# A decoder layer on one core: scores and values' products in blocks of four heads

## What is computed

```
scores = q k^T * scale            (256 x 256)
probs  = softmax(scores)          per row
out_h  = probs v                  (256 x 64)
```

## Time and profile before

| | |
|---|---|
| median of 3 runs | 3596.63 us (3593.33 to 3597.58) |
| the profiled execution | 3596.79 us, its span 3595.0 us, granted TensorE clock 0.993 |
| TensorE busy | 3499.9 us, 97% |
| TensorE weight load | 2955.3 us, 82% |
| VectorE busy | 2361.6 us, 66% |
| ScalarE busy | 2220.9 us, 62% |
| GpSimd busy | 2121.0 us, 59% |

### The profile page before, as it was taken

The page is one execution under the profiler, slowest core; times in us unless marked ns, Lnnn a source line. Parts: engine busy times, 40 slices in busy tenths (PEclk is TensorE's granted clock), DMA queues, the critical chain, the costliest instruction groups (busy, mean ns, idle before and its releaser), DMA issues.

```text
span 3595.0 us, 80997 instructions
## 1 busy us (share of the span) xinstructions
PE 3499.9 (97%) x28992; PEld 2955.3 (82%) x28992; DVE 2361.6 (66%) x7401; ACT 2220.9 (62%) x6442; POOL 2121.0 (59%) x1928
## 2 busy tenths in 40 slices
PE   6899999999999999999999999999999999999997
PEld 5788888888888888888888888888888888888886
DVE  6666667666676666676666666666766666666664
ACT  5666666666666666666665766656666657666563
POOL 5555666555675556665556765566655567655661
PEclk8999999999999999999999999999999999999999
DMA  3100000000000000000000000000000000000000
GB/s 98 37 10 13 10 9 10 10 12 12 7 11 11 9 12 12 6 10 10 12 12 7 13 10 9 12 13 6 10 10 12 12 6 13 10 9 12 13 6 8
DMA packets 46796, 47.44 MB, mean 13 GB/s; under 512 B 8256, under 2 KB 43328, under 8 KB 46400
## 3 DMA queue, kind: packets, MB, share of 16 engines
q1 hardware_dynamic: 45696, 41.99, 4.0%
q10 hardware_dynamic: 704, 0.27, 0.0%
HBM read 33.86 MB, written 8.39 MB: 12 GB/s over the span
## 4 chain that ended last, share of the span: by engine, by line
PE 89%; DVE 6%; issue 2%; POOL 2%; ACT 2%; DMA 0%; ACTq 0%; POOLq 0%; DVEq 0%
PE unit_ps L536 19%; PE pT_ps L648 14%; PE oT_ps L665 14%; PE score_ps L632 11%; PE wo_ps L690 10%; PE unit_ps L546 9%; PE unit_ps L524 9%; DVE x L1021 2%; ACT probs L798 1%; POOL probs L1150 1%; DVE probs L936 1%; PE unit_ps L555 1%; DVE bn L863 1%; DVE x_in L1029 1%; DVE w_lo L851 0%
## 5 line engine op out<-in xcount | busy, mean ns | idle before, releaser
L1150 POOL TENSOR_TENSOR probs<-probs,inv_sum 128x512 f32<-128x512 f32 x1024 | 1062.0, 1041 | 967.3 <-DVE inv_sum L919 967.2
L787 ACT ACTIVATE pT<-pT_ps 128x512 f32<-128x512 f32 x1024 | 605.9, 594 | 135.9 <-PE pT_ps L648 135.4
L798 ACT ACTIVATE probs<-probs,neg_max 128x256 f32<-128x256 f32 x1024 | 508.7, 499 | 277.5 <-DVE probs L936 277.5
L648 PE MATMUL pT_ps<-ident,probs 128*128 128x128 f32 x4096 | 635.3, 280 | 13.0 <-POOL probs L1150 12.4
L648 PEld LDWEIGHTS pT_ps<-ident,probs 128*128 128x128 f32 x4096 | 452.9, 141 | 221.6 <-issue 204.1
L798 ACT ACTIVATE probs<-score_ps,neg_max 128x256 f32<-128x256 f32 x1024 | 476.5, 476 | 179.1 <-DVE neg_max L925 179.1
L665 PE MATMUL oT_ps<-pT,v_sb 128*64 128x256 f32 x4096 | 555.9, 392 | 3.8 <-ACT pT L787 3.5
L936 DVE TENSOR_SCALAR_CACHE_REDUCE probs<-score_ps,mask_add 128x256 f32<-128x256 f32 x1024 | 433.5, 480 | 105.8 <-PE score_ps L632 102.8
L536 PE MATMUL unit_ps<-xs_hi,w_lo 128*128 128x256 f32 x1536 | 460.2, 300 | 8.7 <-DVE swap L972 7.2
L536 PE MATMUL unit_ps<-xs_hi,w_hi 128*128 128x256 f32 x1536 | 436.9, 284 | 0.0
L536 PE MATMUL unit_ps<-xs_lo,w_hi 128*128 128x256 f32 x1536 | 436.3, 284 | 0.0
(11 more groups left out here) (121 smaller groups left out, 8422.2 us busy)
## 6 DMA issues: line engine op xcount, KB each, us to landing
x_in<-dram_x SPq DMA_DIRECT2D x32, 256.0 KB, 2.7
xn<-dram_ctx SPq DMA_DIRECT2D x32, 256.0 KB, 2.7
layer_out<-x SPq DMA_DIRECT2D x32, 256.0 KB, 2.2
swap<-dram_bout SPq DMA_DIRECT2D x32, 128.0 KB, 3.3
rope<-dram_be SPq DMA_DIRECT2D x32, 64.0 KB, 3.1
rope<-dram_we SPq DMA_DIRECT2D x5, 256.0 KB, 2.9
probs<-dram_sk SPq DMA_DIRECT2D x4, 256.0 KB, 4.4
x<-dram_cq SPq DMA_DIRECT2D x4, 256.0 KB, 2.8
```

The costliest lines, as they stand in the source:

```text
L648: last = nc.tensor.transpose(pT_ps[s % 2][:, k * T + t * P:k * T + (t + 1) * P], probs[:, hs % P_BUFS, t, k * P:(k + 1) * P], ident[:])
L787: nc.scalar.activation(flat(pT[:, s % 2, :, :]), pT_ps[s % 2][:], ACT.Copy).then_inc(pT_ready.sem, 1)
L798: last = nc.scalar.activation(dst, src, ACT.Exp, bias=neg_max[:, h % STATS, t:t + 1], scale=1.0 if h < H else -1.0, accum_out=row_sum[:, h ...
L1150: nc.gpsimd.tensor_tensor(weights, weights, inv.unsqueeze(2).to_broadcast([P, NT, T]), ALU.mult).then_inc(probs_ready.sem, 1)
```

## The change

Scores are issued for four heads in a row, in the first slot of each four, and `values` takes the four heads of a group at once, in the slot where the next group's scores are (slots 0, 4, 8, 12, 24, 28, 32, and 17 for the last group of self-attention). `score_ps` and `pT_ps` become four banks `head_ps`: a head's bank holds its scores, and after the exponentials its transposed probabilities. The separate `pT` buffers are gone: ScalarE copies the transposed probabilities back over the head's own `probs`, of which there are 6. So the scores of a head wait for the copy of the head four before it (`pT_ready`), and whoever first writes a `probs` buffer (exponentials of self heads, row maxima of cross heads) waits for the values' product of the head that had it before (`pv_done`). The steps of a head have slots of their own in `AT`, counted within four: row maxima of heads 0, 1, 2 in the first and 3 in the second; exponentials of 0, 1 in the first and 2, 3 in the third; reciprocals and GpSimd's products of 0, 1 in the second and 2, 3 in the third; transposes of 0, 1 at the start of the third and 2, 3 at the start of the fourth. W follows one slot behind the values. All units have new slots and flags, and BI no longer comes right behind scores. Of the removed lines below only some are shown.

```diff
-P_BUFS = 4
+P_BUFS = 6
...
+def in_slot(what, s):
+
+
+    first = s - s % HG
+    return [(head_in(first + j), first + j) for j in range(HG) if AT[what][j] == s % HG and head_in(first + j)]
+
+
+def turned_in(s, end):
+
+
+    first = s - s % HG
+    return [(head_in(first + j), first + j) for j in range(HG)
+            if AT["turned"][j] == 2 * (s % HG) + end and head_in(first + j)]
+
+
 def meets_values(s):
 
 
-    if s % SLOTS == AT["last values"][0]:
-        return head_in(s - 3)
-    if s % 2 or s % SLOTS == AT["last values"][0] + 1:
+    turn, at = divmod(s, SLOTS)
+    if at == AT["last values"][0]:
+        return head_in(turn * SLOTS + DRAIN[0] - HG)
+    if at % HG or at == DRAIN[0]:
         return None
-    return head_in(s - 4)
+    return head_in(s - HG)
+
+
+def leaves(s):
+
+
+    return None if (s - 1) % SLOTS == AT["last values"][0] else meets_values(s - 1)
 
 
 def projects(s):
 
-    if s % SLOTS == AT["last projection"][0]:
-        return head_in(s - 4)
-    pair = meets_values(s - 1)
-    return pair if pair and pair[1] % HG == 2 else None
-
-
-
-
-
-
-
+    turn, at = divmod(s, SLOTS)
+    if at == AT["last projection"][0]:
+        return head_in(turn * SLOTS + DRAIN[0] - HG)
+    behind = s - AT["projected"]
+    return None if behind % SLOTS == AT["last values"][0] else meets_values(behind)
...
 UNITS = {
+    0: [],
+    1: [("Q", 2, 0, NOW), ("V", 0, 0, NOW)],
+    2: [("K", 2, 0, LATE)],
+    4: [],
+    5: [("V", 1, 0, NOW), ("V", 2, 0, NOW), ("Q", 3, 0, LATE)],
+    6: [("L3", 0, -1, LATE)],
+    7: [("K", 3, 0, NOW), ("LG", 0, -1, NOW)],
+    8: [],
+    9: [("V", 3, 0, LATE), ("EX", 0, -1, LATE), ("EX", 1, -1, LATE)],
+    10: [("EX", 2, -1, NOW)],
+    12: [],
+    13: [("EX", 3, -1, LATE)],
+    14: [],
+    15: [("EX", 4, -1, NOW)],
+    17: [("GT", 0, -1, LATE)],
+    18: [("V", 4, 0, LATE), ("K", 4, 0, NOW), ("EX", 5, -1, NOW), ("EX", 6, -1, NOW), ("L2", 0, 0, LATE), ("EX", 7, -1, LATE)],
+    19: [("Q", 4, 0, NOW), ("Q", 5, 0, NOW)],
+    20: [("V", 5, 0, LATE)],
+    21: [("K", 5, 0, NOW), ("BI", 0, -1, NOW)],
+    22: [("Q", 6, 0, NOW)],
+    23: [],
+    24: [("K", 6, 0, LATE)],
+    26: [("V", 6, 0, LATE)],
+    27: [],
+    28: [("L1", 0, 1, LATE), ("K", 7, 0, LATE)],
+    29: [("Q", 0, 1, LATE)],
+    30: [],
+    31: [("K", 0, 1, NOW)],
+    32: [],
+    33: [("Q", 1, 1, NOW), ("V", 7, 0, LATE)],
+    35: [],
...
+    "turn": 1,
+    "split": 2,
+    "statistics 3": 2,
+    "norm 3": 4,
+    "gate table": 9,
+    "context": 16,
+    "mask": 0,
+    "norm 2": [18, 1],
+    "x to x1": 23,
+    "statistics 1": 26,
+    "norm 1": 27,
+    "maxima": [0, 0, 0, 1],
+    "exponentials": [0, 0, 2, 2],
+    "sums": [1, 1, 2, 2],
+    "turned": [4, 4, 6, 6],
+    "projected": 1,
+    "residual 3": 1,
+    "projection first": [14, 27, 31, 35],
...
-        pT = sb("pT", [P, 2, NT, T])
...
-        score_ps = [bank(f"score_ps{i}") for i in range(2)]
-        pT_ps = [bank(f"pT_ps{i}") for i in range(2)]
+
+        head_ps = [bank(f"head_ps{i}") for i in range(HG)]
...
-                back = (0, h - 1) if h else (-1, NH - 1)
-                read = exp_done if 0 < h <= H else max_ready
-                pe.wait_ge(read.sem, read.at(b, back[0], back[1] + 1))
+                back = (0, h - HG) if h >= HG else (-1, NH + h - HG)
+                pe.wait_ge(pT_ready.sem, pT_ready.at(b, back[0], back[1] + 2))
...
+            def turn_probs(b, s, h):
+
+                pe.wait_ge(probs_ready.sem, probs_ready.at(b, 0, h + 1))
                 for k in range(NT):
                     for t in range(NT):
+                        last = nc.tensor.transpose(head_ps[s % HG][:, k * T + t * P:k * T + (t + 1) * P],
+                                                   probs[:, s % P_BUFS, t, k * P:(k + 1) * P], ident[:])
                 last.then_inc(probs_turned.sem, 1)
...
+                g = h // HG
+                pe.wait_ge(pT_ready.sem, pT_ready.at(b, off, h + HG))
+                pe.wait_ge(v_ready.sem, v_ready.at(b, off, g + 1))
+                pe.wait_ge(oT_ready.sem, oT_ready.at(b, off, g))
+                for hl in range(0, HG, 2):
+                    for k in range(NT):
+                        for i in range(2):
+                            last = nc.tensor.matmul(oT_ps[i * HD:(i + 1) * HD, (hl // 2) * T:(hl // 2 + 1) * T],
+                                                    v_sb[:, g % 2, k, (hl + i) * HD:(hl + i + 1) * HD],
+                                                    probs[:, (hs + hl + i) % P_BUFS, k, :], start=k == 0,
+                                                    stop=k == NT - 1, skip_group_check=True)
                 last.then_inc(pv_done.sem, 1)
...
-                    if s % 2 == 0 and head_in(s) and exists(b, 0):
+                    if s % HG == 0 and head_in(s) and exists(b, 0):
                         scores(b, s, head_in(s)[1])
+                        scores(b, s + 2, head_in(s)[1] + 2)
                     if bias_first(s) and exists(b, UNITS[s][0][2]):
                         unit(b, s, 0, *UNITS[s][0][:3])
                     if meets_values(s) and s != AT["last values"][0]:
                         values(b, s)
-                    if head_in(s - 2):
-                        turn_probs(b, s)
+                    for (_, h, _), hs in turned_in(s, 0):
+                        if exists(b, 0):
+                            turn_probs(b, hs, h)
...
-                    act.wait_ge(pv_done.sem, pv_done.at(b, off if g > 1 else off - 1, 2 * ((g - 2) % (2 * NG)) + 2))
+                    act.wait_ge(pv_done.sem, pv_done.at(b, off if g > 1 else off - 1, (g - 2) % (2 * NG) + 1))
...
+            def pT_out(b, s, h):
+
+                act.wait_ge(probs_turned.sem, probs_turned.at(b, 0, h + 1))
+                nc.scalar.activation(flat(probs[:, s % P_BUFS, :, :]), head_ps[s % HG][:],
+                                     ACT.Copy).then_inc(pT_ready.sem, 1)
...
+                    last_group = meets_values(s) if s == AT["last values"][0] else None
+                    if leaves(s) and exists(b, leaves(s)[0]):
+                        oT_out(b, s - 1)
                     for n, (kind, g, off, late) in enumerate(UNITS.get(s - 1, ())):
                         if exists(b, off) and late == LATE:
                             unit(b, unit_ps[unit_bank(s - 1, n) % 2][:], kind, g, off)
-                    if group_ends and s != AT["last values"][0]:
-                        oT_out(b, s)
-                    if here and exists(b, 0):
-                        exponentials(b, s, here[1])
-                    if head_in(s - 2):
-                        pT_out(b, s)
+                    for (_, h, _), hs in in_slot("exponentials", s):
+                        if exists(b, 0):
+                            exponentials(b, hs, h)
+                    for (_, h, _), hs in turned_in(s, 0):
+                        if exists(b, 0):
+                            pT_out(b, hs, h)
...
+                back = buffer_before(s)
+                dve.wait_ge(pv_done.sem, pv_done.at(b, back[0], back[1] // HG + 1))
...
-                    here, summed = head_in(s), head_in(s - 1)
-                    if summed and exists(b, summed[0]):
-                        reciprocal(b, *summed[:2])
-                    if here and s % 2 == 0 and exists(b, 0):
-                        row_maximum(b, s, here[1])
-                        row_maximum(b, s + 1, here[1] + 1)
+                    last_group = meets_values(s) if s == AT["last values"][0] else None
+                    for (_, h, _), hs in in_slot("sums", s):
+                        if exists(b, 0):
+                            reciprocal(b, 0, h)
+                    for (_, h, _), hs in in_slot("maxima", s):
+                        if exists(b, 0):
+                            row_maximum(b, hs, h)
                     for n, (kind, g, off, late) in enumerate(UNITS.get(s - 1, ())):
                         if exists(b, off) and late == LATE:
                             unit(b, unit_ps[unit_bank(s - 1, n) % 2][:], kind, g, off)
-                    pair = meets_values(s)
-                    group_ends = pair and pair[1] % HG == 2 and exists(b, pair[0])
-                    if group_ends and s != AT["last values"][0]:
-                        oT_low(b, s)
+                    if leaves(s) and exists(b, leaves(s)[0]):
+                        oT_low(b, s - 1)
```

More of the change, by code:

```diff
@@ L150 @@
 AT = {
-    "turn": 2,
-    "split": 3,
-    "statistics 3": 4,
-    "norm 3": 5,
+    "turn": 1,
+    "split": 2,
+    "statistics 3": 2,
+    "norm 3": 4,
     "gate weights": 8,
-    "gate table": 8,
-    "context": 11,
-    "mask": 13,
+    "gate table": 9,
+    "context": 16,
+    "mask": 0,
     "statistics 2": [18, 0],
-    "norm 2": [18, 3],
-    "x to x1": 22,
-    "statistics 1": 24,
-    "norm 1": 25,
+    "norm 2": [18, 1],
+    "x to x1": 23,
+    "statistics 1": 26,
+    "norm 1": 27,
     "last values": [17, 0],
     "last projection": [18, 0],
```

(36 more changed lines are left out.)

80 lines of the change are left out of this document (16 added, 64 removed).

## The result

The changed kernel took 3705.32 us, the median of three runs (3701.96 to 3706.17), against 3596.63: a ratio of 1.0304 [1.029, 1.0319], slower. The forecast was 3660, with a range of 3538 to 3745. The profiled execution took 3701.96 us, its span 3700.1.

The account below looks back on a forecast made before the run. TensorE's own work was taken to bound the kernel, at 109.70 us a period; less 3.4 of edges and 1.9 of old waits, plus 7.3 of new, gives 111.7, +64 us over 32 periods: 3660 us, range 3538 to 3745.

Parts of the forecast that it names:

- The gain of the blocks: On TensorE, fewer tile-shape changes around scores and values in blocks of four save net 3.4 us an item.
- EX7: Slot 18: the expert unit EX7 needs EX6's result read first and starts 0.84 us late.
- Waits of 7.3: TensorE's waits on the other engines' written orders sum to 7.3 us an item in place of 1.9.
- EX5 behind V4's copy: Slot 18: EX5 needs V4's bank, which ScalarE copies behind K4's, so it starts 1.36 us late.
- W4: Slot 24: W4 waits for the values' low part, behind K6's low part on VectorE; 0.8 us.
- Q0: Slot 28: Q0 waits for L1's low part, behind ScalarE's copies and VectorE's maxima; 0.7 us.
- slots 34 to 2: GpSimd's queue from head 31 to head 1 takes 10.5 us against TensorE's 8.9; 1.6 us of waits.
- block 4 (Q3, head 7): Q3 waits 0.25 us for V1's copy, and head 7's product comes 0.3 us late.
- block 20 (BI, head 19): BI's bank waits 0.3 us for V5's copy; head 19's product is 0.4 late, its reciprocal behind BI's addition.
- Rival A: Mode changes decide: other engines keep up, waits stay at 1.9 us an item, time 3487 us; chance 0.28.
- Rival B: Only the copies in written order count, GpSimd keeps up: waits 5.7 us an item, 3609 us; chance 0.19.
- Rival C: Four chains, through ScalarE's exponentials and copies, bind every block: waits 10 us, period 114.4, 3747 us; chance 0.13.

Follow-up runs that it names:

- e5: The changed kernel with the gate's table computed on VectorE in slot 8 instead of slot 9; 3689.53 us, ratio 1.0262.
- e10: The changed kernel's blocks of four and instructions, units and steps placed again with VectorE's collisions with GpSimd counted; 3568.97 us, 0.9928 against the kernel before.
- e4: The changed kernel with GpSimd's product with the sine table cut from 512 to 4 columns; 3606.75 us, ratio 1.0033.
- e1: The changed kernel with unit V4 of slot 18 NOW instead of LATE, so its bank is copied before K4's; 3669.46 us, ratio 1.0206.
- e2: The changed kernel with the values' low part computed before K6's low part in VectorE's slot 25; 3676.73 us, ratio 1.0228.
- e11: e10 with the finer weave: scores of two heads, values of two, and again, in seven slots; 3592.42 us, ratio 0.9994.
- e3: The changed kernel with a finer weave: scores of two heads, values of two, and again, in seven slots; 3736.62 us, ratio 1.0392.
- e8: The changed kernel with units, flags and heads' steps placed anew a first time, plus the finer weave of e3; 3635.9 us, ratio 1.0115.

## Why the prediction was right, and where it was short

The direction, the mechanism and the range held; 3660 was 45 us low. By its steps:

- **The gain of the blocks, 3.4 us an item: right.** Work with its edges fell from 107.8 to 104.4. Two of the printed terms are a little off, and move nothing: 35 turns at 0.44 are 15.4, not 15.3, and EX7's parts (0.4 + 1.0 + 0.06 - 0.67) give 0.79, not 0.84.
- **Waits of 7.3: 8.7.** Place by place, predicted and measured in the changed kernel:

| place | predicted | measured |
|---|---|---|
| EX5 behind V4's copy | 1.36 | 1.34 |
| EX7 | 0.84 | 0.90 |
| W4 | 0.8 | 0.83 |
| Q0 | 0.7 | 0.85 |
| slots 34 to 2 | 1.6 | 1.66 |
| block 4 (Q3, head 7) | 0.55 | 0.81 |
| block 20 (BI, head 19) | 0.7 | 0.40 |
| second scores, other blocks | 0.7 | 1.0 |
| EX2 | none | 0.88 |

- **GpSimd's sum of slots 34 to 2** can be read off its timeline. Head 31's product ends at 2084.6, head 1's at 2095.2 (the second of the three in the last row): 10.6, where the prediction had 10.5, with the shuffle's gap at exactly 0.86:

```profile
2083.58 1.04 POOL L1166 TENSOR_TENSOR probs<-probs,inv_sum 128x512 f32<-128x512 f32 x1
2084.58 1.27 POOL L1174 TENSOR_TENSOR swap<-swap,sin_sb 128x512 f32<-128x512 f32 x1
2085.93 1.29 POOL L1178 TENSOR_TENSOR rope<-rope,swap 128x512 f32<-128x512 f32 x1
2088.08 1.28 POOL L1174 TENSOR_TENSOR swap<-swap,sin_sb 128x512 f32<-128x512 f32 x1 [0.86 <-DVE swap L990]
2089.44 1.29 POOL L1178 TENSOR_TENSOR rope<-rope,swap 128x512 f32<-128x512 f32 x1
2090.69 1.29 POOL L1156 TENSOR_TENSOR q_both<-rope,q_both 128x512 fp32r<-128x512 f32 x1
2091.95 1.27 POOL L1156 TENSOR_TENSOR k_lo<-rope,k_hi 128x512 fp32r<-128x512 f32 x1
2093.18 3.22 POOL L1166 TENSOR_TENSOR probs<-probs,inv_sum 128x512 f32<-128x512 f32 x3
```

TensorE waits in there at W7, then at head 1, as its timeline shows. The brackets count from the modelled end of the record before; from start to start, with what follows, the two are late by 1.66 together:

```profile
2092.66 0.39 PE L706 MATMUL wo_ps<-w_hi,oT_lo 128*128 128x256 f32 x1 [0.69 <-DVE oT_lo L1056]
...
2095.27 0.66 PE L665 MATMUL head_ps<-ident,probs 128*128 128x128 f32 x4 [0.34 <-POOL probs L1166]
```

- **The step that was mis-sized** is the sum of waits: 7.3 against 8.7. Of the 1.4, 0.88 is EX2. The prediction has no wait there and prices none of VectorE's small steps; in the kernel before, the cast of the table and the product behind it (L903 and L906 there, L922 and L925 here) took 175 and 162 ns. What it left out is that such a step, moved beside a GpSimd instruction, lasts until that one ends. e5 shows the two steps and the wait go together. The other 0.5 is the net of the other eight places, none off by more than 0.3.
- **The ends** were not priced: +12.7 and -9.0, 4 in all; the 2.0 a period was counted 32 times, where 30 periods carry it. 1.37 x 30 + 3.7 - 4 = 41 us make 3660 into 3701; the profiled execution took 3702. That the two ends and the two periods too many nearly cancel is luck. The later start is over the 10 us that the prediction named as something it has not priced, and no run here looks into it.
- **Rival A** (the mode changes decide, 3487) is out as the change stood: waits were far over 5.3. Its condition holds, though: e10 has 4.5 and is faster. **Rival B** is out by e4. **Rival C** is out: TensorE's waits name no exponential of ScalarE in the whole run, and the period stayed under its 114.4.
- **The signs named in advance** came: the period (113.07, just past the 111 to 113), 24 score records in 1.66, 16 of values in 1.88, EX5, GpSimd without a gap but one.

What stays open: no run undoes the units' placement and keeps the four-head blocks otherwise as they were; e1, e2, e5 and e10 only show that placement and order alone are worth 136 us. Nor does one place the units of the kernel before anew with its blocks of two; e11 is the nearest, and its weave is not the same.

## What to carry to other kernels

Fewer, longer blocks on the bound engine give what its starts say, 3.4 us an item here, but they make the chains of the other engines start together, and a strict order on each of these turns that into waits of twice the gain, though none is over two thirds busy. Walk each queue in its written order and price every place where one engine's instruction stands ahead of what the bound engine needs: three such edits, of a line or two each, took 1.1, 0.9 and 0.4 us off the period, and they added up. Price VectorE's casts and norm steps within SBUF, and its steps with two inputs there, by what GpSimd does at that moment. Undoing a merge cost less than its edges in all three trials here (e3, e8, e11).

## What the runs showed of the hardware

**Some VectorE steps stand until the GpSimd instruction beside them ends, however short they are; others do not.** Steps over 16 and 4 elements (L906, L922, L925) took 0.96 to 1.25 us in the mean beside GpSimd's products and 0.16 to 0.18 otherwise, and ended within 0.04 us of GpSimd's end. The kernel before has it too, in two steps of its own gate (1071 and 1020 ns); only the place decides whether it costs. But the reciprocal between them (L923) took 0.15 with GpSimd busy throughout, as the timelines at e5 show, and the sum L1009, one of whose two inputs is a bank of PSUM, 174 ns beside GpSimd in 31 of 32 times.

The Trainium skill, SBUF — State Buffer, section SBUF: two separate sides, says that the port pair which VectorE and GpSimd share is an exclusive lock, held for a whole instruction, and that on VectorE's side it is taken by a step "with two SBUF inputs" (against a GpSimd instruction that reads SBUF) or by one in a mode that uses both of VectorE's ports. By that rule L906 and L925 (two inputs) must stand until GpSimd's end, and the trace agrees. The cast of L922 has one input in SBUF, and so comes under the second half: the same page, section Who interferes with whom, counts copies, casts and `tensor_scalar` among those that can enter such a mode. Its 0.8 us of standing fits; in which mode it ran no trace shows.

**The norm is as much a victim.** Its step over `x`, a TENSOR_SCALAR with one tensor input, took 1260 ns in the mean and 861 with the sine product cut short (e4), where the same step over `x_in`, which never meets GpSimd there, took 410. In e10, where half of the steps over `x_in` meet it, their mean is 653. The two-element step of the mask (L1109) went from 148 ns before the change to 1014.

**Added edges cost a quarter to two fifths of themselves.** 2.4 us of mode changes an item showed as 1.0 (e3), 0.83 (e8) and 0.64 (e11). In e3 and e11 waits fell by 1.5 and 1.7 at the same time. That the edges take the place of waits for a bank's copy is my reading of where these fell.
